# Graph network layers, one core: third tail column in a group of scatters, another place for the row table, weights split on ScalarE and GpSimd

## Chip, cores and metric

The kernel runs on one core of a Trainium2 chip. The metric is the device time of one launch in microseconds, the median of several runs. The engines are TensorE (PE), VectorE (DVE), ScalarE (ACT), GpSimd (POOL) and SyncE (SP), with 16 DMA engines that move data for all of them.

## What is computed

A graph has 3125 nodes with 64 features and 100000 weighted edges `src -> dst`, sorted by `dst`. Four graph layers follow each other, each on `h = relu(layernorm(x))`, and each adds its result to `x`:

```python
# layer 0: three propagations with deg^-1/2 on both sides, mean of four terms
msgs = x[row] * norm[:, None]
x = jax.ops.segment_sum(msgs, col, num_segments=num_nodes)
# layer 1: weighted mean over neighbours, two linear maps
msg = feat[src] * weight[:, None]
neigh_sum = jax.ops.segment_sum(msg, dst, num_segments=n)
rst = feat @ W_self.T + b_self + (h_neigh @ W_neigh.T + b_neigh)
# layer 2: Chebyshev filters of order 3 with symmetric normalisation, GRU gates
Z = sigmoid(_cheb_conv(X, src, dst, w, Wxz, bxz, n) + ...)
# layer 3: attention over the edges, 4 heads
att = exp(clip(einsum('ehd,ehd->eh', q, k), -10, 10))
out = segment_sum((att / attNorm)[:, :, None] * v, rows)
```

## The kernel before

**The idea.** The edges are turned into two dense matrices of 3200 x 3200 in device memory, one of edge counts and one of summed weights. After that every propagation is a product with one of them (`NPROP = 6` of these), and the attention layer uses the counts as well.

**First stage, tables.** `table` is an array of pairs (weight, count), one per cell, in tiles of 128 destination nodes (T = 25). The edges lie as columns of 128: edge `128 c + p` is in partition p of column c. A group is G = 10 columns; there are NG = 79 groups. Two edges of one cell may not be added by two lanes of the same scatter, so for each group DVE finds which edges are the last of their cell, and PE sums over the others:

- `make_row` (PE, L1136) spreads a group's keys over a row of 1280.
- `compare_own` (DVE, L772 to L784) compares each of the ten columns with the row and writes `equal`, then copies the weight parts (L780) and writes `is_row` (L782) and `is_tile` (L784).
- `compare_tail` (DVE, L764) compares the last TAIL = 2 columns of the group before with this group's row, all 1280 wide. What was still to be summed of these columns is carried on to this group.
- `add_up` (PE, L1119 to L1128) multiplies `equal` with the weight parts (three bf16 parts of an f32 weight, and a one for the count), and adds the carried amounts with `equal_tail` (L1128).
- `choose_cells` (DVE, L795 to L821) takes the sums and writes the cell numbers (L813) and amounts into one of SLOTS = 12 slots.
- `scatter` (POOL, L1350) issues one indirect DMA with addition per column.

DVE runs the loop one group behind itself: tail compare and own compare of group g, then the cells of group g-1. Over all groups but the first, `compare_tail` is called 78 times. After 14 and after 38 groups some other work of DVE stands between (first block L859 to L870, layer norm and weights).

**Order of the scatters.** Two scatters in flight may not touch the same cell. The first G - TAIL columns of a group are its body, the last TAIL its tail, each with its own semaphore:

```python
pool.wait_ge(body_landed, 16 * BODY * g)
scatter(slot, range(TAIL), body_landed)
previous_landed(g)          # waits for tail_landed, 16 * TAIL * g
scatter(slot, range(TAIL, BODY), body_landed)
scatter(slot, range(BODY, G), tail_landed)
```

So with TAIL = 2 a group begins when the body before it has landed, two scatters after the last of that body was issued, and its third column goes out when the tail before it has landed.

**Zeroing.** The table has to be zeroed tile by tile before it is added to. ACT issues four DMAs a tile (`zero_tile`, L504), the first ZEROED_AHEAD = 2 tiles at once one after the other, the rest as groups start.

**Splitting the table.** When enough groups have landed, ACT loads a tile (L526, 3.2 MB), splits it into weights and counts (L534, L537) and stores both (L546, 1.6 MB each). Tile 23 is copied by DVE into the ring (L946) and not only stored.

**Second stage, products.** SP streams pieces of the matrices (1.28 MB each) through a ring of five slots (`stream`, L452) and into places where they stay (`keep`, L458), PE multiplies (L1288, L1231, L1243), and DVE and ACT finish each block of columns. The ring lies where the first stage keeps keys, weights and parts, so SP waits with all of this for `scratch_read`, which DVE sets after its last group. The first two propagations go over blocks of four tiles each as far as tiles are stored.

**Third stage, attention.** Scores, exponentials, clip, product with the counts, sum over values: from about 1990 us on.

**The weights at the start.** The edge data come in rows and are transposed by PE (`turn_edges`, L1077): tiles, keys, rows, then weights. DVE copies each out of PSUM (`edges_of`, L713), and the copy is what frees the PSUM bank for PE (`edges_read`). The weights are copied to `w_e` and split into three bf16 parts in `parts` on DVE: cast, subtract, cast, subtract, cast (L735, L736, L742, L743, L756), with ones and a comparison for the count column (L757, L758).

Of the kernel before, what the change touches and what calls it, by code (L numbers as in the profile page):

```python
# [17 lines left out]
P = 128  # L18
# [6 lines left out]
NR = T * P  # L25
LAST = N - (T - 1) * P
G = 10
GE = G * P
NG = -(-E // GE)
ECP = NG * G  # L30
EDGE_TILES = -(-E // P)
WHOLE_TILES = E // P
REST = E - WHOLE_TILES * P
CHUNK_TILES = -(-ECP // P)
TAIL = 2
OWN_AT = [sum(G - i for i in range(j)) * P for j in range(G + 1)]
CELLS = NR * NR
TILE_CELLS = NR * P
ZEROED_AHEAD = 2
# [31 lines left out]
ALU = mybir.AluOpType  # L71
# [3 lines left out]
BF16 = mybir.dt.bfloat16  # L75
# [85 lines left out]
def carver(area):  # L161

    used = [0]

    def take(shape, dt):
        view, used[0] = carve(area, used[0], shape, dt)
        assert used[0] <= area.shape[1]
        return view

    return take  # L170


def tables_and_products(nc, c, k, sb, table, weights_dram, counts_dram, x_in, src, dst, edge_weight,
# [3 lines left out]
    def sem(name):  # L177
        return c.enter_context(nc.semaphore(name))
# [9 lines left out]
    ZEROS = 2 * NR // 4  # L188
# [9 lines left out]
    equal = [take([P, OWN_AT[G]], BF16) for b in range(2)]  # L198
    masks = take([P, P + GE], F32)
    take = carver(scaled_area)  # L200
    equal_tail, is_row = take([P, 2, TAIL, GE], BF16), take([P, 2, G, P], BF16)
    cells = k["held"][:, 0:2 * NR].rearrange("p (s c two) -> p s c two", c=P, two=2)
# [69 lines left out]
    needs_ready, group_started, group_taken = sem("needs_ready"), sem("group_started"), sem("group_taken")  # L272
    row_ready, first_keys = sem("row_ready"), sem("first_keys")
    masks_set, compared, tail_compared = sem("masks_set"), sem("compared"), sem("tail_compared")
    equal_ready, degrees_added = sem("equal_ready"), sem("degrees_added")
# [126 lines left out]
    with nc.Block() as block:  # L402
        @block.sync
        def _(sp):
# [5 lines left out]
            for tile, dram, landed in ((src_i, src, edges_landed), (dst_i, dst, edges_landed),  # L410
                                       (w_raw, edge_weight, weights_landed)):
                sp.dma_start(tile[0:LAST_ROWS, FILLED],
                             dram[FILLED * P * P:WHOLE_TILES * P].rearrange("(t e) -> t e", e=P)).then_inc(landed, 16)
                sp.dma_start(tile[LAST_ROWS:LAST_ROWS + 1, FILLED, 0:REST],
                             dram[WHOLE_TILES * P:E].rearrange("(a e) -> a e", a=1)).then_inc(landed, 16)
            sp.wait_ge(small_cleared, 3)
            small = [(k["x"][:, 0:T - 1, :], x_in[0:(T - 1) * P].rearrange("(t p) f -> p t f", p=P)),
# [12 lines left out]
            for to, frm in ((k["w_self"][row, :], b_self), (bias_in[row, 0:D], b_neigh),  # L430
                            (k["cheb0"][row, 0:D], bxz), (bias_in[row, D:2 * D], bhz),
                            (k["cheb0"][row, D:2 * D], bxh), (bias_in[row, 2 * D:3 * D], bhh)):
                sp.dma_start(to, frm.rearrange("(a f) -> a f", a=1)).then_inc(small_landed, 16)


            def tiles_stored(last_tile):
# [57 lines left out]
        def _(act):  # L494
# [5 lines left out]

            def zero_tile(t):
                for quarter in range(4):
                    cols = slice(quarter * ZEROS, (quarter + 1) * ZEROS)
                    act.dma_start(blocks[bass.ds(t, 1), :, cols].rearrange("a p c -> (a p) c"), zeros  # L504
                                  ).then_inc(quarter_zeroed, 16)
                act.wait_ge(quarter_zeroed, 64 * t + 64)
                act.sem_inc(tiles_zeroed, 1)

            for t in range(ZEROED_AHEAD):
                zero_tile(t)  # L510
            act.wait_ge(needs_ready, 4)
# [166 lines left out]
        def _(dve):  # L678
            steps = [0]

            def link(ins):

                steps[0] += 1
                ins.then_inc(dve_step, 1)
                dve.wait_ge(dve_step, steps[0])
# [10 lines left out]
            nc.vector.memset(masks[:, P:P + GE], 1.0).then_inc(masks_set, 1)  # L696
            link(nc.vector.memset(parts[:], 0.0))

# [12 lines left out]
            def edges_of(to, banks, n):  # L711
# [21 lines left out]
                                    ALU.is_ge, ALU.mult).then_inc(extremes_ready, 1)  # L733
            edges_of(w_e, totals, 4)
            link(nc.vector.tensor_copy(parts[:, :, 0], w_e[:]))  # L735
            link(nc.vector.tensor_tensor(w_e[:], w_e[:], parts[:, :, 0], ALU.subtract))  # L736
            dve.wait_ge(extremes_turned, 2)
# [3 lines left out]
                                    ).then_inc(extremes_ready, 1)  # L741
            link(nc.vector.tensor_copy(parts[:, :, 1], w_e[:]))  # L742
            link(nc.vector.tensor_tensor(w_e[:], w_e[:], parts[:, :, 1], ALU.subtract))  # L743
            nc.vector.tensor_scalar(schedule[:, 0], tiles_iota[0:1, :], float(LOAD_EVERY), float(LOADS_FROM),
# [10 lines left out]
            nc.vector.tensor_copy(tile_numbers, tiles_iota[:]).then_inc(masks_set, 1)  # L755
            nc.vector.tensor_copy(parts[:, :, 2], w_e[:])  # L756
            nc.vector.memset(parts[:, 0:WHOLE_TILES, 3:4], 1.0)  # L757
            link(nc.vector.tensor_scalar(parts[:, WHOLE_TILES, 3:4], partition[:], float(REST), None, ALU.is_lt))  # L758
            dve.wait_ge(masks_set, 4)
# [8 lines left out]

            def compare_own(g, b, more=True):

                for j in range(G):
                    ins = nc.vector.scalar_tensor_tensor(  # L772
                        equal[b][:, OWN_AT[j]:OWN_AT[j + 1]], key_row[b][:, j * P:GE], keys[:, bass.ds(g * G + j, 1)],
                        own_mask[:, 0:GE - j * P], ALU.is_equal, ALU.mult, accum_out=later[:, b, j:j + 1])
                if more:
                    ins = nc.vector.tensor_copy(keys_now[:, b], keys[:, bass.ds((g + 2) * G, G)])
                ins.then_inc(compared, 1)
                dve.wait_ge(row_ready, g + 2 if more else NG)
                edges = bass.ds(g * G, G)
                nc.vector.tensor_copy(parts_g[:, b], parts[:, edges, :])  # L780
                nc.vector.tensor_tensor(keys_rel[:, b], keys[:, edges], dummy[:], ALU.subtract)
                nc.vector.tensor_tensor(is_row[:, b], row_numbers.unsqueeze(1).to_broadcast([P, G, P]),  # L782
                                        dst_row[:, edges].unsqueeze(2).to_broadcast([P, G, P]), ALU.is_equal)
                nc.vector.tensor_tensor(is_tile[:, b], tile_numbers.unsqueeze(1).to_broadcast([P, G, T]),  # L784
                                        dst_tile[:, edges].unsqueeze(2).to_broadcast([P, G, T]), ALU.is_equal
                                        ).then_inc(equal_ready, 1)
# [40 lines left out]
            dve.wait_ge(row_ready, 1)  # L827
            compare_own(0, 0)
            dve.wait_ge(row_ready, 2)
# [497 lines left out]
        def _(pool):  # L1327
# [15 lines left out]
            nc.gpsimd.iota(partition[:], pattern=[[0, 1]], base=0, channel_multiplier=1,  # L1343
                           allow_small_or_imprecise_dtypes=True).then_inc(pool_step, 1)
            pool.wait_ge(needs_ready, 4)
            pool.wait_ge(dummies_zeroed, 16)
# [385 lines left out]
```

## Time and profile before

| | us |
|---|---|
| median of 3 runs | 2415.12 (2412.22 to 2417.41) |
| the profiled execution | 2415.37 |
| its span, first to last instruction | 2413.6 |
| DVE busy | 1786.2 (74%) |
| POOL busy | 1563.6 (65%) |
| PE busy | 1359.5 (56%) |
| ACT busy | 636.7 (26%) |

The span is what the trace shows of one execution; 1.8 us lie around it. Busy shares are means over three stages with different limits, so the text goes by stretches. DMA issues are not counted as busy for SP and ACT. In the rows, "ring", "resident", "scaled" and "held" are large areas of on-chip memory that hold different tables in different stages; `table` is the cell array.

### The profile page before, as it was taken

What the parts mean: (1) busy time and instruction counts of PE and PEld (TensorE: products, weight loads), DVE (VectorE), ACT (ScalarE), POOL (GpSimd) and SP (SyncE); (2) the same over time, 40 slices, a digit from 0 to 9 for tenths busy, and PEclk for the clock granted to TensorE, in tenths of its full rate; (3) what the DMA queues carried; (4) which work ended last, traced back from release to release, by engine and by line L of the source; (5) the groups of instructions that cost most, each with busy time, mean ns of one, the idle gap of its engine ahead of it and who ended that gap; (6) DMA issues with size and microseconds to landing.
All of it is one profiled execution on the core that took longest, in us unless ns stands there. A gap on an engine that the chain in (4) does not pass through costs nothing. (4 is left out here: it accounts for less than half of the span.)

```text
span 2413.6 us, 41312 instructions
## 1 busy us (share of the span) xinstructions
PE 1359.5 (56%) x13050; PEld 756.0 (31%) x13050; DVE 1786.2 (74%) x3954; ACT 636.7 (26%) x1822; POOL 1563.6 (65%) x1191
## 2 busy tenths in 40 slices
PE   2332223332332332333232577599999979999998
PEld 2222222222222222222222122143434443333334
DVE  8999999999999999999999000132321358999996
ACT  0000000012232331322111111010000237888884
POOL 1788888888888888888888777400000037888884
PEclk6555555555555555555555888799999988999997
DMA  5566666645666656664554999899998865333331
GB/s 202 164 163 192 183 170 164 164 109 164 181 167 198 164 164 204 175 167 116 142 124 80 339 372 346 300 375 360 395 397 298 323 179 160 106 104 104 106 107 50
DMA packets 253738, 481.44 MB, mean 199 GB/s; under 512 B 130710, under 2 KB 140093, under 8 KB 243933
## 3 DMA queue, kind: packets, MB, share of 16 engines
q1 hardware_dynamic: 113180, 229.09, 27.7%
q10 hardware_dynamic: 26000, 245.78, 25.5%
q0 software_dynamic: 114480, 5.67, 12.2%
q8 instruction: 33, 0.54, 0.1%
q14 instruction: 45, 0.36, 0.0%
HBM read 312.54 MB, written 167.91 MB: 199 GB/s over the span
## 5 line engine op out<-in xcount | busy, mean ns | idle before, releaser
L1350 POOL DMA_INDIRECT table<-held x782 | 1216.6, 1556 | 331.8 <-issue 305.9
L772 DVE SCALAR_TENSOR_TENSOR resident<-banks,ring,resident 128x1280 bf16<-128x1280 f32 (+9 forms) x790 | 694.3, 946 | 0.3 <-DVE ring L758 0.3
L1136 PE MATMUL banks<-ident,held 128*128 128x128 f32 x790 | 189.2, 426 | 866.0 <-DVE held L784 831.5
L1136 PEld LDWEIGHTS banks<-ident,held 128*128 128x128 f32 x790 | 157.6, 225 | 873.4 <-DVE held L784 838.1
L1545 DVE TENSOR_TENSOR att<-att,banks_d 128x1024 f32<-128x1024 f32 (+1 forms) x350 | 365.9, 1085 | 36.6 <-POOL att L1610 29.8
L1610 POOL TENSOR_SCALAR att<-att 128x1024 f32<-128x1024 f32 (+1 forms) x350 | 320.3, 934 | 85.8 <-ACT att L1513 85.8
L534 ACT ACTIVATE held<-held 128x128 f32<-128x128 f32 x575 | 172.0, 301 | 764.1 <-DMA weights_dram<-held 732.3
L1288 PE MATMUL banks<-ring,scaled 128*64 128x512 f32 x1120 | 297.4, 623 | 71.6 <-DMA ring<-counts_dram 50.0
L1513 ACT ACTIVATE att<-banks_d 128x1024 f32<-128x1024 f32 (+1 forms) x350 | 302.3, 915 | 79.8 <-PE banks_d L1633 79.8
L1398 POOL DMA_DIRECT2D parts_dram<-scaled x7 | 5.5, 779 | 380.1 <-DVE scaled L984 379.9
L764 DVE SCALAR_TENSOR_TENSOR scaled<-banks,ring,resident 128x1280 bf16<-128x1280 f32 x156 | 235.7, 1549 | 16.8 <-PE banks L1136 10.9
L1633 PE MATMUL banks_d<-held 96*128 (+2 forms) x700 | 170.2, 366 | 10.6 <-ACTq L1504 9.8
L1648 PE MATMUL banks_d<-att,v_tile 128*32 128x512 f32 (+1 forms) x1400 | 172.0, 567 | 0.5 <-DVE att L1545 0.5
L1288 PEld LDWEIGHTS banks<-ring,scaled 128*64 128x64 f32 x1120 | 91.3, 142 | 244.5 <-issue 186.8
L1119 PE MATMUL banks<-ring,resident 128*128 128x6 bf16 x4345 | 132.3, 167 | 24.5 <-DVE held L784 22.7
L1119 PEld LDWEIGHTS banks<-ring,resident 128*128 128x128 bf16 x4345 | 124.1, 104 | 33.9 <-DVE held L784 23.0
L517 ACT ACT_TABLE_LOAD x1 | 1.3, 1283 | 470.5 <-DMA table<-acc 470.5
L782 DVE TENSOR_TENSOR scaled<-banks,ring 128x1280 bf16<-128x1280 f32 x79 | 117.2, 1484 | 0.0
L1633 PEld LDWEIGHTS banks_d<-held 96*128 (+1 forms) x700 | 54.0, 99 | 182.0 <-issue 130.0
L534 ACT ACTIVATION_READ_ACCUMULATOR held<-held (+1 forms) x575 | 107.7, 187 | 0.0
L1640 PE MATMUL banks_d<-ident,count 128*128 128x128 f32 x625 | 102.6, 282 | 1.6 <-DVE att L1545 1.0
L1640 PEld LDWEIGHTS banks_d<-ident,count 128*128 128x128 f32 x625 | 79.2, 144 | 29.1 <-issue 8.9
(227 smaller groups left out, 1455.7 us busy)
## 6 DMA issues: line engine op xcount, KB each, us to landing
table<-acc ACTq DMA_DIRECT2D x100, 800.0 KB
held<-table ACTq DMA_DIRECT2D x24, 3200.0 KB
ring<-weights_dram SPq DMA_DIRECT2D x60, 1280.0 KB, 13.6
ring<-counts_dram SPq DMA_DIRECT2D x54, 1280.0 KB, 12.1
weights_dram<-held ACTq DMA_DIRECT2D x25, 1600.0 KB
counts_dram<-c_tile ACTq DMA_DIRECT2D x24, 1600.0 KB, 14.3
count<-counts_dram SPq DMA_DIRECT2D x150, 256.0 KB, 2.7
table<-held POOLq DMA_INDIRECT x782
```

Source lines behind the costliest of these rows:

```text
L534: ins = nc.scalar.activation(w_rows[:, s // PIECE, s % PIECE], cells[:, s, :, 0], ACT.Copy, accum_out=deg_parts[:, s, bass.ds(t, 1)])
L764: ins = nc.vector.scalar_tensor_tensor(equal_tail[:, b, i, :], key_row[b], keys[:, bass.ds(g * G - TAIL + i, 1)], all_mask, ALU.is_equal, ...
L772: ins = nc.vector.scalar_tensor_tensor(equal[b][:, OWN_AT[j]:OWN_AT[j + 1]], key_row[b][:, j * P:GE], keys[:, bass.ds(g * G + j, 1)], own_ ...
L1119: nc.tensor.matmul(sums, equal[b][:, at:at + P], parts_g[:, b, j, :], start=False, stop=True, skip_group_check=True)
L1136: ins = nc.tensor.transpose(key_row[b][:, j * P:(j + 1) * P], keys_now[:, b, j:j + 1].to_broadcast([P, P]), k["ident"][:])
L1288: ins = nc.tensor.matmul(sums, xs[:, prop % 2, s], rows_for(s), start=i < 2 and (prop != 1 or n == NC - 1), stop=True, skip_group_check=True)
L1350: nc.gpsimd.indirect_dma_start(out=table, out_offset=bass.IndirectOffsetOnAxis(ap=cell[:, slot, j:j + 1], axis=0), in_=amount[:, slot, j, ...
L1513: nc.scalar.activation(att[:, j, pairs[f], 0:W], scores[:, pairs[f], 0:W], ACT.Exp).then_inc(scores_read[f], 1)
L1545: ins = nc.vector.tensor_tensor(att[:, j, pairs[f], 0:W], att[:, j, pairs[f], 0:W], times, ALU.mult)
L1610: nc.gpsimd.tensor_scalar(att[:, j, pairs[f], 0:W], att[:, j, pairs[f], 0:W], HI, LO, ALU.min, ALU.max).then_inc(clipped[f], 1)
L1633: ins = nc.tensor.matmul(scores[:, hd, 0:W], k6[:, hd, bass.ds(t * P, P)], q6[:, hd, bass.ds(ci * BANK, W)], start=True, stop=True)
L1640: ins = nc.tensor.transpose(count_t[j % 3][:, s * P:(s + 1) * P], count[:, j, s, :], k["ident"][:])
```

## The change

TAIL goes from 2 to 3: `compare_tail` compares three columns per group, the body has seven scatters and the tail three, and the carried arrays have three columns. `is_row` moves from the area "scaled" to "resident", which makes room for the larger `equal_tail`. The copy of the weights and the casts into `parts` go to ACT, the subtracts, the ones and the comparison to POOL. PE's bank is freed by ACT after its second copy. The zeroing of tiles 0 and 1 goes to SP, ahead of its small loads.

```diff
-TAIL = 2
+TAIL = 3
...
+    is_row = take([P, 2, G, P], BF16)
     take = carver(scaled_area)
-    equal_tail, is_row = take([P, 2, TAIL, GE], BF16), take([P, 2, G, P], BF16)
+    equal_tail = take([P, 2, TAIL, GE], BF16)
...
+            sp.wait_ge(zeros_ready, 1)
+            for t in range(ZEROED_AHEAD):
+                for quarter in range(4):
+                    cols = slice(quarter * ZEROS, (quarter + 1) * ZEROS)
+                    sp.dma_start(table[0:CELLS].rearrange("(t p c) two -> t p (c two)", p=P, c=NR)[t, :, cols], zeros
+                                 ).then_inc(first_zeroed, 16)
             sp.wait_ge(small_cleared, 3)
...
+            sp.wait_ge(first_zeroed, 64 * ZEROED_AHEAD)
+            sp.sem_inc(tiles_zeroed, ZEROED_AHEAD)
...
-                act.wait_ge(quarter_zeroed, 64 * t + 64)
+                act.wait_ge(quarter_zeroed, 64 * t - 64 * (ZEROED_AHEAD - 1))
                 act.sem_inc(tiles_zeroed, 1)
 
-            for t in range(ZEROED_AHEAD):
-                zero_tile(t)
+            act.wait_ge(edges_turned, 4)
+            turned_weights = totals.rearrange("p a r -> p (a r)")[:, 0:ECP]
+            nc.scalar.copy(w_e[:], turned_weights).then_inc(weights_cast, 1)
+            act.wait_ge(parts_cleared, 1)
+            nc.scalar.copy(parts[:, :, 0], turned_weights).then_inc(weights_cast, 1)
+            act.wait_ge(weights_cast, 2)
+            act.sem_inc(edges_read, 1)
+            for n in range(1, 3):
+                act.wait_ge(weights_left, n)
+                nc.scalar.copy(parts[:, :, n], w_e[:]).then_inc(weights_cast, 1)
+            act.wait_ge(tiles_zeroed, ZEROED_AHEAD)
             act.wait_ge(needs_ready, 4)
...
-            edges_of(w_e, totals, 4)
-            link(nc.vector.tensor_copy(parts[:, :, 0], w_e[:]))
-            link(nc.vector.tensor_tensor(w_e[:], w_e[:], parts[:, :, 0], ALU.subtract))
...
-            link(nc.vector.tensor_copy(parts[:, :, 1], w_e[:]))
-            link(nc.vector.tensor_tensor(w_e[:], w_e[:], parts[:, :, 1], ALU.subtract))
...
-            nc.vector.tensor_copy(parts[:, :, 2], w_e[:])
-            nc.vector.memset(parts[:, 0:WHOLE_TILES, 3:4], 1.0)
-            link(nc.vector.tensor_scalar(parts[:, WHOLE_TILES, 3:4], partition[:], float(REST), None, ALU.is_lt))
...
+                if first:
+                    dve.wait_ge(ones_parted, 2)
+                    dve.wait_ge(weights_cast, 4)
                 nc.vector.tensor_copy(parts_g[:, b], parts[:, edges, :])
...
-            compare_own(0, 0)
+            compare_own(0, 0, first=True)
...
+            pool.wait_ge(parts_cleared, 1)
+            nc.gpsimd.memset(parts[:, 0:WHOLE_TILES, 3:4], 1.0).then_inc(ones_parted, 1)
+            pool.wait_ge(ones_parted, 1)
+            nc.gpsimd.tensor_scalar(parts[:, WHOLE_TILES, 3:4], partition[:], float(REST), None, ALU.is_lt
+                                    ).then_inc(ones_parted, 1)
+            for n in range(2):
+                pool.wait_ge(weights_cast, n + 2)
+                nc.gpsimd.tensor_tensor(w_e[:], w_e[:], parts[:, :, n], ALU.subtract).then_inc(weights_left, 1)
             pool.wait_ge(needs_ready, 4)
```

On DVE, ahead of the first compare, before (names: "held" has the schedule here, "ring" the parts of the weights):

```order
L753 SCALAR_TENSOR_TENSOR held<-banks,held 1x25
L755 COPY banks<-held 128x25
L756 CAST ring<-ring 128x790
L757 MEMSET ring 128x781
L758 TENSOR_SCALAR ring<-held 128x1
L772 SCALAR_TENSOR_TENSOR resident,held<-banks,ring,resident 128x1280
```

and now:

```order
L769 TENSOR_SCALAR held<-held 1x25
L771 SCALAR_TENSOR_TENSOR held<-banks,held 1x25
L773 COPY banks<-held 128x25
L787 SCALAR_TENSOR_TENSOR resident,held<-banks,ring,resident 128x1280
L787 SCALAR_TENSOR_TENSOR resident,held<-banks,ring,resident 128x1152
```

The cast and the two fills (like five more rows further up) are gone from DVE; the first compare follows the small schedule steps directly.

On DVE within a group, from `is_tile` to the cell numbers, before (`x2` is the tail compare):

```order
L784 TENSOR_TENSOR held<-banks,ring 128x250
L764 SCALAR_TENSOR_TENSOR scaled,held<-banks,ring,resident 128x1280 x2
L795 TENSOR_TENSOR deg_in<-deg_in,banks 128x25
L797 TENSOR_REDUCE held<-banks 128x20
L802 SCALAR_TENSOR_TENSOR held<-held 128x4
L807 TENSOR_TENSOR held<-held 128x2
```

and now:

```order
L802 TENSOR_TENSOR held<-banks,ring 128x250
L779 SCALAR_TENSOR_TENSOR scaled,held<-banks,ring,resident 128x1280 x3
L813 TENSOR_TENSOR deg_in<-deg_in,banks 128x25
L815 TENSOR_REDUCE held<-banks 128x20
L820 SCALAR_TENSOR_TENSOR held<-held 128x6
L825 TENSOR_TENSOR held<-held 128x3
```

One tail compare is added, and the carry steps have six and three elements in place of four and two.

## Rows read from the trace of the kernel before

**Rows 1.** The page's slices: busy tenths and GB/s in 40 equal slices.
```profile
DVE  8999999999999999999999000132321358999996
...
DMA  5566666645666656664554999899998865333331
GB/s 202 164 163 192 183 170 164 164 109 164 181 167 198 164 164 204 175 167 116 142 124 80 339 372 346 300 375 360 395 397 298 323 179 160 106 104 104 106 107 50
```

**Rows 2.** The page's costliest groups: busy us, mean ns of one, idle before.
```profile
L1350 POOL DMA_INDIRECT table<-held x782 | 1216.6, 1556 | 331.8 <-issue 305.9
L772 DVE SCALAR_TENSOR_TENSOR resident<-banks,ring,resident 128x1280 bf16<-128x1280 f32 (+9 forms) x790 | 694.3, 946 | 0.3 <-DVE ring L758 0.3
...
L764 DVE SCALAR_TENSOR_TENSOR scaled<-banks,ring,resident 128x1280 bf16<-128x1280 f32 x156 | 235.7, 1549 | 16.8 <-PE banks L1136 10.9
```

**Rows 3.** Timeline of POOL: start us, us, instruction, idle time before it.
```profile
51.92 1.85 POOL L1350 DMA_INDIRECT table<-held  x1 [47.42 <-issue]
...
96.19 1.55 POOL L1350 DMA_INDIRECT table<-held  x1 [2.97 <-issue]
...
1330.56 1.55 POOL L1350 DMA_INDIRECT table<-held  x1 [1.82 <-DMA table<-held]
...
1527.45 1.55 POOL L1350 DMA_INDIRECT table<-held  x1 [6.09 <-issue]
1529.30 1.55 POOL L1350 DMA_INDIRECT table<-held  x1 [0.30 <-issue]
...
1549.43 1.55 POOL L1350 DMA_INDIRECT table<-held  x1 [3.72 <-issue]
```

**Rows 4.** Timeline of DVE, the cell numbers of groups 2, 77 and 78.
```profile
94.39 0.17 DVE L813 TENSOR_TENSOR held<-held 128x10 f32 x1 [0.17 <-DVE held L810]
...
1303.23 0.17 DVE L813 TENSOR_TENSOR held<-held 128x10 uint32<-128x10 f32 x1
...
1321.83 0.17 DVE L813 TENSOR_TENSOR held<-held 128x10 uint32<-128x10 f32 x1
```

**Rows 5.** Timeline of DVE, first and last step of the block between groups.
```profile
273.18 1.82 DVE L859 TENSOR_REDUCE stat<-x_nodes 128x25 f32<-128x1600 f32 x1
...
282.13 0.23 DVE L870 TENSOR_TENSOR halves_sum<-ident 128x64 f32<-128x64 f32 x1
```

**Rows 6.** Timeline of SP: the first loads of the counts, merged.
```profile
1321.89 92.10 SPq L452 DMA_DIRECT2D ring<-counts_dram  x20
1414.10 23.18 SPq L458 DMA_DIRECT2D resident<-counts_dram  x4
1441.99 66.85 SPq L452 DMA_DIRECT2D ring<-counts_dram  x14
```

**Rows 7.** Windows: length, busy us of each engine, PE clock, DMA share, GB/s.
```profile
1300.00:1555.00 255.00, 149.37 (x689) 52.13 (x691) 39.92 (x96) 35.45 (x157) 182.44 (x118) 0.76 0.96 314
1555.00:1920.00 365.00, 348.72 (x1862) 153.43 (x1860) 96.21 (x253) 37.65 (x73) 0.00 (x0) 0.99 0.94 352
```

**Rows 8.** Timeline around PE's wait for tile 23.
```profile
1528.80 0.35 ACTq L526 DMA_DIRECT2D held<-table  x1
...
1545.49 1.98 PE L1288 MATMUL banks<-ring,scaled 128*64 128x512 f32 x4 [15.77 <-DVE ring L946]
```

**Rows 9.** Timeline of DVE: a wait for PE in group 1, and two tail compares.
```profile
66.89 0.18 DVE L795 TENSOR_TENSOR deg_in<-deg_in,banks 128x25 f32<-128x25 f32 x1 [2.46 <-PE banks L1128]
...
1304.63 1.54 DVE L764 SCALAR_TENSOR_TENSOR scaled<-banks,ring,resident 128x1280 bf16<-128x1280 f32 x1
...
1306.10 1.55 DVE L764 SCALAR_TENSOR_TENSOR scaled<-banks,ring,resident 128x1280 bf16<-128x1280 f32 x1
```

**Rows 10.** Timeline of DVE: the first cast of the weights, the first compare.
```profile
22.25 1.48 DVE L735 CAST ring<-ring 128x790 bf16<-128x790 f32 x1
...
33.37 1.55 DVE L772 SCALAR_TENSOR_TENSOR resident<-banks,ring,resident 128x1280 bf16<-128x1280 f32 x1 [0.29 <-DVE ring L758]
```

**Rows 11.** A copy on ACT (timeline) and the clip on POOL (the page's groups).
```profile
1504.33 3.08 ACT L537 COPY c_tile<-held 128x3200 f32<-128x3200 f32 x1
...
L1610 POOL TENSOR_SCALAR att<-att 128x1024 f32<-128x1024 f32 (+1 forms) x350 | 320.3, 934 | 85.8 <-ACT att L1513 85.8
```

More of the change, by code:

```diff
@@ L273, in tables_and_products @@
     row_ready, first_keys = sem("row_ready"), sem("first_keys")
+    parts_cleared, ones_parted = sem("parts_cleared"), sem("ones_parted")
+    weights_cast, weights_left = sem("weights_cast"), sem("weights_left")
+    first_zeroed = sem("first_zeroed")
     masks_set, compared, tail_compared = sem("masks_set"), sem("compared"), sem("tail_compared")
@@ L696, in _ @@
             nc.vector.memset(masks[:, P:P + GE], 1.0).then_inc(masks_set, 1)
-            link(nc.vector.memset(parts[:], 0.0))
+            nc.vector.memset(parts[:], 0.0).then_inc(parts_cleared, 1)
             dve.wait_ge(edges_landed, 16 * 6)
@@ L767, in compare_tail, with compare_own @@
                 ins.then_inc(tail_compared, 1)
-            def compare_own(g, b, more=True):
+            def compare_own(g, b, more=True, first=False):
                 for j in range(G):
```

## The prediction

> **What bounds the kernel now.** I read the page's slices first: VectorE (DVE) is busy at 9 tenths up to the 22nd of 40 slices, and the DMA share jumps to 9 where DVE falls to nothing [rows 1]. A slice is 60 us, so both happen near 1320 us. The costliest groups say what runs until then: 782 scatters on GpSimd (POOL), the compares on DVE [rows 2]. I then took three timelines.
>
> First, the scatters. One is 1.55 us and the next starts 0.30 after its end [rows 3], 1.856 us in all, so a group of ten takes 18.56 us. The first starts at 51.92, the last but one at 1549.43 [rows 3], so POOL is done near 1553. 782 x 1.856 is 1451 us, so of these 1501 only some 50 are waits beyond the 0.30. They lie in two places: four before 140 us (the second is the one at 96.19), and twelve from 1330.56 to 1549.43, in nearly every case one a group, up to 6.09 us [rows 3]. Between them POOL never waits.
>
> Second, DVE. The sum that writes a group's cell numbers (L813), on which its scatters wait, is at 94.39 for group 2 and 1303.23 for group 77 [rows 4]. Less a block of other work in between (273.18 to 282.36, 9.2 us [rows 5]) that is (1208.8 - 9.2) / 75 = 16.0 us a group. So DVE gains 2.56 us a group on POOL.
>
> Third, the handover. DVE's last such sum is at 1321.83 [rows 4], and SyncE issues the first load of the count matrix at 1321.89 [rows 6]: the ring that these loads fill holds the keys that DVE compares, so **the stream begins when DVE has finished**, while POOL still scatters. From there DMA is the limit: its share is 0.96 in 1300:1555 at 314 GB/s [rows 7], by slice 339, 372, 346 and 300 GB/s, against 395 and 397 in later slices without scatters [rows 1]. After 1555 DMA (share 0.94, 352 GB/s) and TensorE (PE, 348.72 of 365 us busy) are both nearly full [rows 7]. Only once do they stand still for another reason: PE waits 15.77 us, until 1545.49, for DVE's copy (L946) of tile 23, which waits for that tile's load, issued at 1528.80 [rows 8]. That load waits for scatters. These 15.8 us are all the slack between the two paths: POOL's path ends last there, DVE's and the stream's come 16 us before it.
>
> **The change, part by part.**
>
> *Third tail column on DVE.* compare_tail runs 78 times (156 compares, two each [rows 2]) and gets one more compare of 128x1280. Their starts lie 1.47 us apart (1304.63, 1306.10) although each is shown as 1.55 [rows 9], so it costs 78 x 1.47 = 114.7 us of DVE. For group 1 DVE waits 2.46 us for PE at 66.89 [rows 9], which hides 1.1 of the 1.47 (PE's ten more matmuls a group take some of it back; they are small and overlap: I take 0.4). The carry steps have 6 elements in place of 4, nothing. Sum +113.6 us; with 1.55 for each it would be +120. The group takes 16.0 + 1.47 = 17.47 us, still under POOL's 18.56, by 1.09. DVE's lead at its end shrinks to some five groups, so the twelve slots never hold it up.
>
> *The weights.* Off DVE go a copy, three casts and two subtracts of 790 columns and two short fills, eight steps before the first compare at 33.37; the first cast takes 1.48 us from 22.25 on [rows 10]. Some 9 us of DVE go, and the small steps left between them (1.5 us) need PE's answers and PE's row of keys (ten transposes) as before. PE also waits until ScalarE (ACT) has copied the weights twice. No copy of 790 columns is there on ACT; 3200 take 3.08 us [rows 11], so 0.8 us each, or double if half of it is a fixed part. The first of them can start where DVE's copy did, a microsecond before 22.25. 21.2 + 2 x 0.8 (to 1.6) + 2.4 for the row gives a first compare at 25.2 to 26.8: I take **-7 us** (between -6 and -8.5). Two subtracts on POOL and two casts on ACT must then be done when DVE copies the parts, after its ten compares of the group, which by the mean of 0.946 us [rows 2] come to 9 us. POOL clips 1024 columns in 0.93 us [rows 11]; two inputs may cost it twice as much, so 2 x 1.6 + 2 x 0.8 and some handovers are near 6 us: hidden. If a POOL step took 4 us, some 2 us would come back.
>
> *Zeroing of tiles 0 and 1 by SyncE*: the same 8 DMAs go out on another queue, behind the edges, and no longer one tile after the other. Both tiles are 6.4 MB, 21 us even at the 300 GB/s of the slowest of the four slices named above, and the first scatter starts at 51.92 [rows 3]: nothing. The small loads queued behind them are not used until 273 us [rows 5]. *is_row moves* inside on-chip memory, same shape: nothing, as all work there stays on DVE and PE.
>
> *Scatters.* The first comes 7 - 1.5 = 5.5 us earlier. Group 2 was already waited for on DVE's side (L813 at 94.39, scatter at 96.19 [rows 3, 4]); it moves to about 94.39 - 7 + 1.47 + 0.4 + 1.47 = 90.7, so 3.7 earlier only. In each group the waits for the body and for the tail now come three scatters after the last of these, not two: 1.86 us more cover. That takes up to 3.7 from the third and fourth wait. Of the twelve late waits the six before 1428 (the first is that at 1330.56, together 14.8 us beyond the 0.30 [rows 3]) stand beside the stream, which isn't there yet, and should go; the six after can lose 11 at most, and I take half. POOL ends near 1553 - 3.7 - 3.7 - 14.8 - 5 = 1526, within 1520 to 1545.
>
> Here a rule speaks against the third column. The body's last scatter is the eighth of ten, so the group that starts at 1527.45 sends it at 1527.45 + 7 x 1.856 = 1540.44, and the next group may go on at 1549.43 [rows 3]: from its end a landing took 7.4 us there, and no more than the 4.0 of two scatters and a gap where POOL never waits. The Trainium skill (DMA: Bandwidth & Descriptors, Anatomy of one DMA) puts a DMA started by GpSimd at a fixed 2.0 us or so. By that rule two scatters of distance would always do, and the scatter term would be 0; the trace agrees with it from 140 to 1330 us and contradicts it at both ends.
>
> *The stream.* It now starts at 1321.9 - 7 + 113.6 = **1428**. From 1321.9 up to PE's restart at 1545.5 it must bring 20 + 4 + 11 full pieces of 1.28 MB (the 14 issued from 1441.99 hold 3 short ones), 1.5 MB of short ones, one for c_tile and the first 0.96 of tile row 5: 48.6 MB [rows 6]. Besides, each tile costs a load and a store of 3.2 MB. From 1428 to 1525 at 360 GB/s, amid the four slices, DMA moves 35 MB; two loads and two stores take 12.8, so 22 MB of stream. Left are 26.4, with a load and a store 33 MB, at the 395 GB/s of a slice without scatters [rows 1] 83 us: PE restarts at 1608 in place of 1545.5, **+62 us**. Since tile 24 is then long there, PE's small waits behind it and the last loads beside it should fall away, -5. All later work shifts with it: PE has 16 us of idle in the next 365 [rows 7].
>
> **Sum:** -7 + 113.6 on DVE is 106.6; 15.8 of it is the old slack; some 29 come from less traffic beside the stream (12.8 MB of tile traffic done before 1428) and the higher rate once the scatters end; 5 behind it: +57. The profiled execution took 2415.4 (span 2413.6 and 1.8 around it), 0.3 over the median of 2415.1. Forecast 2415.1 + 57 = **2472 us**.
>
> **Rivals.**
> - *Full delay.* The stream keeps its old pace, 314 to 350 GB/s with the same gaps: +106.6 - 15.8 = +91, 2506. For: DMA's share is full already at the low rates. Against: a quarter of the old traffic in that stretch is gone. 0.13.
> - *More is caught up.* PE uses the 16 us of idle after 1555 and DMA runs at 395 all along: 67.8 MB in 172 us is a restart at 1600, +54, less 16 and 5: +33, 2448. Against: both engines would have to be full at once. 0.13.
> - *DVE becomes the bound of the scatters too.* The margin is 1.09 us a group. If the new group took 19.5 us (PE's answers later, POOL and DVE in each other's way), the stream would start at 1428 + 78 x 2.0 = 1584, with hardly any scatter or tile traffic beside it: 48.6 MB at 395 in 123 us put PE's restart at 1707 and the end at 2415 + 162 - 5 = 2572. Against: one compare more needs nothing new of PE. 0.03.
> - *Faster:* POOL's end alone sets the end, and the stream catches up in full. Then the 28 us that the scatters end earlier are the gain, less the part that falls behind: 2390 to 2413. Decides if 48.6 + 12.8 MB move between 1428 and 1517, 690 GB/s; the highest slice shows 397 [rows 1]. 0.03.
> - *No change* (within 0.2%, about what runs of this kernel can tell): the stream's slack is far larger than the 16 us seen, because DMA moves the same bytes at a higher rate when they are asked for later. PE's 149.37 busy us in 1300:1555 [rows 7] would nearly fit into what is left, the bytes don't. 0.02.
>
> **How the numbers follow.** Forecast 0.66. The range takes in both neighbours: low 2440 (a bit under 2448, for a start 2 us better and POOL's end at 1520), high 2508 (full delay). Outside are 0.03 above, 0.05 below, and some of the neighbours' spread. Slower 0.95, same 0.02, faster 0.03.
>
> **What would show it.** 234 tail compares; SyncE's first count load near 1428; the last scatter near 1525; no wait over 3 us of POOL from 140 to 1428; PE's restart with tile row 5 near 1608, waiting for the ring and not for DVE's copy of tile 23; everything from there 365 us long as before. If PE still waits there for DVE's copy, the stream had slack that I don't see, and the time is near or under the old one. If DVE's group is over 18.6 us, the third rival holds.

## The result, and the profile after

The changed kernel takes **2507.6 us** (median of 4, 2506.53 to 2509.18) against 2413.7 (2408.99 to 2417.41) for the kernel before: ratio 1.0387, 95% interval 1.0375 to 1.0399. Slower, as forecast, but by 94 us where 57 were forecast. That is the value of the rival "full delay" (2506), and it lies 0.4 us inside the upper end of the range (2508), which was set by that rival. The profiled execution's span is 2505.2 (before 2413.6).

The page's slices of the changed kernel (a slice is 62.6 us), as in [rows 1]:

```profile
DVE  8999999999999999999999800032221157999996
...
DMA  6566576546656657554442399998999785333332
GB/s 194 158 198 169 158 210 158 158 105 187 181 158 194 174 158 210 158 158 105 105 105 1 77 360 381 342 372 331 395 397 346 291 261 150 106 105 105 107 107 52
```

VectorE is busy up to the 23rd slice now. New is the hole ahead of the stream: 1 GB/s in the 22nd slice and 77 in the 23rd, which ends with the stream's first pieces. No tile is loaded, split or stored there.

The costliest groups of the changed kernel, as in [rows 2]:

```profile
L1376 POOL DMA_INDIRECT table<-held x782 | 1212.7, 1551 | 311.2 <-issue 286.2
...
L787 DVE SCALAR_TENSOR_TENSOR resident<-banks,ring,resident 128x1280 bf16<-128x1280 f32 (+9 forms) x790 | 694.1, 945 | 3.7 <-PE banks L1154 3.7
L779 DVE SCALAR_TENSOR_TENSOR scaled<-banks,ring,resident 128x1280 bf16<-128x1280 f32 x234 | 350.4, 1547 | 14.9 <-PE banks L1154 10.9
```

234 tail compares cost 350.4 us in place of 235.7 for 156: 114.7 more, the very sum forecast.

The timeline of VectorE, cell numbers of groups 2, 76, 77 and 78, as in [rows 4] (groups are numbered from 0, so 78 is the last):

```profile
92.42 0.17 DVE L831 TENSOR_TENSOR held<-held 128x10 f32 x1 [0.17 <-DVE held L828]
...
1407.76 0.17 DVE L831 TENSOR_TENSOR held<-held 128x10 uint32<-128x10 f32 x1
1424.77 0.17 DVE L831 TENSOR_TENSOR held<-held 128x10 uint32<-128x10 f32 x1
1427.76 0.17 DVE L831 TENSOR_TENSOR held<-held 128x10 uint32<-128x10 f32 x1
```

The last is 105.9 us later than before. A group takes (1407.76 - 92.42 - 9.2) / 74 = 17.65 us. Counted back from the last one, the 1303.23 of [rows 4] was group 76's and not 77's, so the group before took 1208.8 - 9.2 over 74, 16.2 us, and the margin to POOL is now 0.9 us.

The timeline of SyncE, the stream, as in [rows 6]:

```profile
1427.82 128.43 SPq L465 DMA_DIRECT2D ring<-counts_dram  x20
1556.36 14.97 SPq L471 DMA_DIRECT2D resident<-counts_dram  x4
1575.17 51.47 SPq L465 DMA_DIRECT2D ring<-counts_dram  x14
```

It begins where forecast (1428), but the first 20 pieces take 128.4 us in place of 92.1. Beside them four tiles are now loaded and four stored; before, it was two loads and one store.

The timeline of ScalarE's queue, tile loads (the last ahead of the hole, then tiles 20 to 23) and the step between them:

```profile
1251.93 0.35 ACTq L549 DMA_DIRECT2D held<-table  x1
...
1427.67 0.21 ACT L592 COPY w_neigh<-banks 128x64 f32<-128x64 f32 x1 [137.05 <-PE banks L1180]
1428.72 0.41 ACTq L549 DMA_DIRECT2D held<-table  x1
1464.13 0.35 ACTq L549 DMA_DIRECT2D held<-table  x1
1499.30 0.35 ACTq L549 DMA_DIRECT2D held<-table  x1
...
1533.31 0.35 ACTq L549 DMA_DIRECT2D held<-table  x1
```

This is what the forecast missed. Between tile 19's split and tile 20's load, ScalarE's program has a block of other work: two copies of layer weights that PE turns when VectorE's groups are over, then the square root of the degrees. ScalarE waited 137 us for it. In the kernel before, the same wait was 27.2 us, and tile 20's load came out 12 us behind it, when enough scatters had landed; the block didn't hold it, since run 10, without the block ahead of it, has the load at 1333.82. The timeline of ScalarE before:

```profile
1321.74 0.21 ACT L569 COPY w_neigh<-banks 128x64 f32<-128x64 f32 x1 [27.23 <-PE banks L1162]
...
1333.69 0.35 ACTq L526 DMA_DIRECT2D held<-table  x1
```

The timeline of GpSimd, the starts of groups from 1428 on, as in [rows 3]:

```profile
1444.03 1.54 POOL L1376 DMA_INDIRECT table<-held  x1 [8.46 <-issue]
...
1454.80 1.54 POOL L1376 DMA_INDIRECT table<-held  x1 [5.53 <-DMA table<-held]
...
1485.80 1.54 POOL L1376 DMA_INDIRECT table<-held  x1 [12.80 <-DMA table<-held]
...
1526.11 1.54 POOL L1376 DMA_INDIRECT table<-held  x1 [9.16 <-issue]
...
1554.94 1.54 POOL L1376 DMA_INDIRECT table<-held  x1 [10.63 <-issue]
1556.79 1.55 POOL L1376 DMA_INDIRECT table<-held  x1 [0.30 <-issue]
```

There are five waits of 5.5 to 12.8 us where there were six of 2.1 to 6.1, although each has a scatter more of cover. The four waits at the start did not shrink either: 15.4 us in sum, before 12.8. POOL ends at 1558, not at 1526.

PE's restart with tile row 5, the copy of tile 23 that it waits for (the timeline, as in [rows 8]) and the windows, as in [rows 7] (length, busy us of PE, PE's weight loads, DVE, ACT and POOL, PE clock, DMA share, GB/s):

```profile
1632.16 4.46 PE L1261 MATMUL banks<-ring,scaled 128*64 128x512 f32 x10 [2.91 <-DMA ring<-counts_dram]
...
1636.72 3.49 DVE L964 COPY ring<-held 128x3200 f32<-128x3200 f32 x1 [38.25 <-PE banks L1261]
...
1640.31 11.52 PE L1306 MATMUL banks<-ring,scaled 128*64 128x512 f32 x40 [3.68 <-DVE ring L964]
```

```profile
1427.00:1640.00 213.00, 128.51 (x493) 42.81 (x490) 16.25 (x37) 35.43 (x157) 72.27 (x47) 0.80 1.01 363
...
1640.00:2010.00 370.00, 354.35 (x1882) 155.25 (x1884) 97.64 (x252) 37.65 (x73) 0.00 (x0) 0.99 0.94 354
```

PE still waits for DVE's copy, but only for its 3.7 us; the copy itself waited 38 us for PE's earlier products (L1261), and the last of these waited for a piece of the stream. The forecast's sign for slack in the stream, PE waiting for the copy, was badly chosen: the copy waits in its turn. It is the stream that sets the restart, 94.8 us later than before. From there to the end it is 864.9 us (before 868.1).

The same stretch of the kernel before, from the start of its stream to its restart, as windows:

```profile
1321.00:1545.00 224.00, 134.61 (x496) 44.02 (x493) 16.27 (x37) 35.45 (x157) 160.99 (x105) 0.78 1.05 353
```

224 us at 353 GB/s are 79.1 MB; 213 at 363 are 77.3. **The stretch carries nearly the same bytes as before**, with four tile loads and four stores in each; some 2 MB are fewer.

### The profile page after: what moved, and what is told of

Read it like the earlier page. It is cut to its first block and busy times, and to the rows that moved or that the text cites. A ratio compares the mean times of both kernels' runs of the same rounds, so it can differ in the third digit from the quotient of the medians.

```text
span 2505.2 us, 43099 instructions
## 1 busy us (share of the span) xinstructions
PE 1364.8 (54%) x13830; PEld 771.5 (31%) x13830; DVE 1893.7 (76%) x4102; ACT 647.0 (26%) x1827; POOL 1567.9 (63%) x1195
## 5 line engine op out<-in xcount | busy, mean ns | idle before, releaser
L779 DVE SCALAR_TENSOR_TENSOR scaled<-banks,ring,resident 128x1280 bf16<-128x1280 f32 x234 | 350.4, 1547 | 14.9 <-PE banks L1154 10.9
L1137 PE MATMUL banks<-ring,resident 128*128 128x6 bf16 x4345 | 128.9, 167 | 25.2 <-DVE held L802 25.2
L800 DVE TENSOR_TENSOR resident<-banks,ring 128x1280 bf16<-128x1280 f32 x79 | 117.0, 1481 | 0.0
L625 ACT COPY scaled<-banks 128x512 f32<-128x512 f32 (+1 forms) x35 | 18.9, 539 | 312.0 <-PE banks L1306 312.0
```

The source lines that it names most:

```text
L779: ins = nc.vector.scalar_tensor_tensor(equal_tail[:, b, i, :], key_row[b], keys[:, bass.ds(g * G - TAIL + i, 1)], all_mask, ALU.is_equal, ...
L1137: nc.tensor.matmul(sums, equal[b][:, at:at + P], parts_g[:, b, j, :], start=False, stop=True, skip_group_check=True)
```

## The experiments

The common idea behind them is that VectorE's end starts the stream, and that what lies beside the stream sets how fast it catches up.

**1. ScalarE's block later** (the changed kernel, one edit):

```diff
+            pass_on(T // 4 - 2, 3)
+            pass_on(T // 4 - 1, 0)
             act.wait_ge(turned_ready, 1)
...
-            pass_on(T // 4 - 2, 3)
-            for j in range(2):
-                pass_on(T // 4 - 1, j)
+            pass_on(T // 4 - 1, 1)
```

> The changed kernel, but ScalarE's wait for VectorE's last group (turned_ready, deg_ready, three small steps) stands after two more tiles are passed on, so that loads and stores of tiles 20 and 21 are not queued behind it. Theory A: in the changed kernel these loads (first one issued at 1428.7, when VectorE ended) fell into the stream and slowed it; here the load of tile 20 is issued near 1325, SyncE's first 20 pieces take 100 us in place of 128, PE's restart after its early pieces moves from 1640 to about 1612, and the time is 2480 us (2470 to 2490). Rival B: the stream beside scatters is slow whatever ScalarE does, and the loads only change places: 2503 to 2510.

Measured: 2484.3 us (2483.85 to 2486.64), ratio 1.0289 (1.0272 to 1.0306). Its timeline of ScalarE, then its windows and PE's restart:

```profile
1324.08 0.35 ACTq L549 DMA_DIRECT2D held<-table  x1
...
1379.66 0.35 ACTq L549 DMA_DIRECT2D held<-table  x1
...
1427.60 0.21 ACT L594 COPY w_neigh<-banks 128x64 f32<-128x64 f32 x1 [9.30 <-PE banks L1180]
1438.95 0.39 ACTq L549 DMA_DIRECT2D held<-table  x1
...
1502.97 0.35 ACTq L549 DMA_DIRECT2D held<-table  x1
```

```profile
1427.00:1617.00 190.00, 127.35 (x492) 44.37 (x490) 16.65 (x38) 14.27 (x55) 70.63 (x46) 0.82 0.96 335
```

```profile
1616.96 10.03 PE L1306 MATMUL banks<-ring,scaled 128*64 128x512 f32 x30 [3.68 <-DVE ring L964]
```

Two tiles are loaded and two stored in what was the hole: 190 us at 335 GB/s are 63.7 MB, 13.6 fewer than in the changed kernel. PE restarts at 1617, POOL's late waits are 4.6 us at most and its last scatter ends at 1525, the value forecast. The first 20 pieces take 106.5 us (100 were expected). The hold of ScalarE's queue cost 23.3 us of the 94. The rate fell with the bytes: 13.6 MB at 363 GB/s would be 37 us, and only 23 came back.

**2. Only tile 20's load ahead of the block** (the changed kernel; `pass_on` of tile 19 is taken apart):

```diff
+            split_done(KEPT_OUT - 4)
+            load(KEPT_OUT - 3)
             act.wait_ge(turned_ready, 1)
...
-            pass_on(T // 4 - 2, 3)
+            store(KEPT_OUT - 4, 1)
+            split(KEPT_OUT - 3, 0, 2 * (T // 4 - 2) + 2)
```

> The changed kernel with that same edit: tile 20's load near 1324 in place of 1428.7, but tile 19's store, tile 21's load and tile 20's store still behind the block, as in the changed kernel. 3.2 of the 12.8 MB that the earlier move took out of the stream's stretch. If the loss is a matter of bytes moved into that stretch, a quarter to a third of the 23.3 us comes back: 2499 to 2503. Rival: the chain of load, split and store per tile sets the pace of tile 23 and so counts by tiles, one of two is half of it: 2494 to 2498.

Measured: 2498.97 us (2498.12 to 2501.47), ratio 1.0348 (1.0334 to 1.0362). By its windows:

```profile
1427.00:1633.00 206.00, 125.16 (x486) 41.79 (x488) 16.81 (x38) 35.45 (x157) 69.56 (x46) 0.81 1.01 360
```

74.2 MB, 3.1 fewer than in the changed kernel, and 8.6 us less time, for one of the four transfers (3.2 MB each) that run 1 moved. That is 37% of run 1's gain, between the two expectations (2499 to 2503 by bytes, 2494 to 2498 by tiles), just below the first. The restart, at 1632.90, is 7.4 us earlier, a third of run 1's 23.3. So the bytes explain it better than the count of tiles, but the two are not told apart cleanly.

**3. Two columns again, all else as changed** (`TAIL = 2` in the changed kernel).

> The changed kernel with TAIL back at 2: the parts of the change on the weights, the row table and the zeroing alone. Theory: first compare 3.5 us earlier as in the changed kernel (29.9 against 33.4), first scatter near 47, and as the path over the scatters sets PE's restart here, the gain comes through: 2409 to 2412 us. Rival: the gain is lost in the wait of group 2 or later: 2413 to 2415.

Measured: 2405.8 us (2404.72 to 2406.93), ratio 0.9959 (0.9945 to 0.9973): 3 us better than the best expected. The third column is the whole loss, 101.8 us against this run; what else was changed leaves 10 us of gain. Its stream starts only 1 us earlier than in the kernel before (1320.95), 106.9 us ahead of the changed kernel's, but tile 23 is loaded at 1520.32 in place of 1528.80, and PE's 15.8 us of waiting for its copy [rows 8] are 3.7 (more of PE's waiting now lies ahead of it, for pieces of the ring):

```profile
1543.17 13.81 PE L1306 MATMUL banks<-ring,scaled 128*64 128x512 f32 x49 [3.68 <-DVE ring L964]
```

The restart is only 2.3 us earlier; most of the gain falls behind it (861.7 us to the end, before 868.1). Which of the parts gives that, no run separates.

**4. Three columns alone** (the kernel before with `TAIL = 3` and `is_row` moved).

> The kernel before with TAIL = 3 and the row table moved to make room, nothing else. Theory: all of the loss is here: VectorE ends 3.5 us later than in the changed kernel (1431), time 2509 to 2513 us. Rival: the weights' new places cost something later on, then this is under 2505.

Measured: 2521.2 us (2518.39 to 2523.66), ratio 1.0442 (1.0424 to 1.0459). Outside what was expected: VectorE's end is at 1439.3, 11.5 us later than in the changed kernel. 3.65 of it are the first compare (33.52 for 29.87). Two waits with no releaser stand in its timeline of VectorE, at the first instruction of a round of twelve groups, and not in the changed kernel's:

```profile
939.11 1.55 DVE L765 SCALAR_TENSOR_TENSOR scaled<-banks,ring,resident 128x1280 bf16<-128x1280 f32 x1 [3.70 <-issue]
...
1157.45 1.55 DVE L765 SCALAR_TENSOR_TENSOR scaled<-banks,ring,resident 128x1280 bf16<-128x1280 f32 x1 [7.42 <-issue]
```

These 11.1 us and the 3.65 are 3.3 more than the 11.5; what gives the 3.3 back is open, and so is what the two waits are. From PE's restart (1651.45) to the end it is 865.0 us, as in the changed kernel.

**5. Three columns compared, scatters split 8 + 2** (`BODY = G - 2` in the changed kernel): the cover that the third column buys is given back.

> The changed kernel (three columns compared), but the scatters' own split is two columns again: body of eight, tail of two. Theory: the scatters are not what the end waits for in the changed kernel, so the time stays at 2505 to 2510 us; the waits before group starts grow by up to 1.86 us each, four early ones and five late ones, and the last scatter ends 5 to 17 us later than 1558. Rival: the waits are set by how fast DMA works off the scatters, not by the distance: same waits in sum, same end of the scatters within 3 us.

Measured: 2506.3 us (2504.27 to 2507.39), ratio 1.0378 (1.0361 to 1.0396): the same. POOL's waits beyond 0.30, without the first, add up to 71.6 us against 59.4, and its last scatter starts at 1566.28, 9.5 us later; the restart is at 1637.66, no later at all (1640.31 in the changed kernel). Of the 12.2 us of longer waits 2.3 lie before 180 us, the rest beside the stream. So the cover works on POOL, and POOL is off the path.

**6. The reverse: two compared, split 7 + 3** (`BODY = G - 3` in the kernel before).

> The kernel before (two columns compared), but the scatters are split as in the changed one, body of seven and tail of three, so the waits come three scatters after the last of their kind. Left out: what protects the third last column of a group against the same cell in the next group, so some sums may be lost; the number and size of the scatters is the same. Theory (a wait is a landing time less the distance): each of the waits, four early and about ten late, shrinks by up to 1.86 us; the last scatter ends 10 to 20 us before 1553, tile 23 is loaded earlier, and as PE's restart was set by that: 2402 to 2410 us. Rival (DMA works the scatters off at its own pace beside the stream): end of the scatters within 4 us, 2413 to 2416 us.

Measured: 2409.8 us (2407.61 to 2413.58), ratio 0.9982 (0.9973 to 0.9992). The last scatter starts 15 us earlier (1536.03) and tile 23's load 11 us earlier:

```profile
1517.74 0.35 ACTq L526 DMA_DIRECT2D held<-table  x1
```

PE's wait for the copy is gone from its timeline; now it waits for the ring:

```profile
1542.44 8.45 PE L1288 MATMUL banks<-ring,scaled 128*64 128x512 f32 x30 [4.75 <-DMA ring<-counts_dram]
```

That is what the longer distance alone gains in this kernel: about 5 us, with no third compare to pay for.

**7. One column compared** (the kernel before; `for i in range(TAIL - 1, TAIL)`, the left-out row zeroed once).

> The kernel before with one tail compare per group in place of two. Left out: the carry from the second last column (its equal_tail is zero throughout). Theory: VectorE ends 113 us earlier, near 1209, and the stream starts there, but PE's restart still waits for tile 23, which the scatters set (1545); the time moves by under 15 us: 2402 to 2416. Rival: VectorE's end sets the time as it stands, in this direction too: 2320 to 2380.

Measured: 2408.2 us (2403.86 to 2409.64), ratio 0.9969 (0.9958 to 0.998). The time is as expected, VectorE's end is not: 1308, not 1209. From group 57 on it waits for the slots:

```profile
917.78 0.18 DVE L795 TENSOR_TENSOR deg_in<-deg_in,banks 128x25 f32<-128x25 f32 x1 [1.96 <-POOLq L1367]
...
936.42 0.18 DVE L795 TENSOR_TENSOR deg_in<-deg_in,banks 128x25 f32<-128x25 f32 x1 [3.42 <-POOLq L1367]
```

These two are 18.6 us apart, POOL's pace. With twelve slots VectorE can't be further ahead. The stream starts 13.7 us earlier, and PE then waits 37.84 us for tile 23.

**8. GpSimd's ones later** (run 3, with a wait for the turned edges ahead of the fill): `pool.wait_ge(edges_turned, 4)`.

> The changed kernel with TAIL = 2 and GpSimd's fill of the ones (2.69 us at 7.5 in the changed kernel, beside a VectorE step of 2.96 us that took 0.63 before) put behind the transposes of the edges. Theory: GpSimd's fill holds VectorE up; the step is 0.63 again, the first compare comes 2.0 to 2.3 us earlier (27 in place of 29.1), and of it 1 to 2.3 us arrive at the end: 2403 to 2405 us against 2405.8. Rival: the step is slow for another reason (DMA writing the edges), no change. Either way GpSimd's fill then lies beside other VectorE steps and may stretch one of these.

Measured: 2405.1 us (2403.8 to 2405.86), ratio 0.9961 (0.9947 to 0.9974). The first compare is at 26.89 in place of 29.11 (25.2 to 26.8 were forecast); the total is not told apart from run 3.

**9 and 10. The block later with two columns**: run 1's edit on run 8 and on the kernel before.

> The version with two tail columns and the late fill of ones, with the move of ScalarE's block that gave 23 us with three. With two columns ScalarE waited 36.3 us for the block's product, until 1320.73, and issued tile 20's load at once behind it, at 1322.03. Theory (the load is held by the block): it is issued some 10 us sooner, near 1310, before the stream begins at 1318.7; a part of its 3.2 MB leaves the stretch of the stream, up to 8 us, of which the waits of PE for the ring can take back most: 2397 to 2404. Rival (nothing of it is on the path, since PE's restart hangs on later tiles): 2404 to 2406.

> The kernel before with the same move of ScalarE's block alone. There ScalarE waited 27.2 us, until 1321.74, but tile 20's load went out only at 1333.69, 11 us behind the block: it waited for scatters, so the block held nothing up. Theory: the time is the same, 2412 to 2417, and the 23 us of the same edit in the changed kernel are a cost that only the third compare brings. Rival (the hold was part of the old time too): 2400 to 2410.

Both expectations were wrong. Measured: 2460.0 us (2456.2 to 2461.84), ratio 1.0184 (1.0171 to 1.0198), for run 9, and 2471.3 us (2470.9 to 2472.27), ratio 1.0232 (1.0218 to 1.0246), for run 10. The timelines of ScalarE, of SyncE and of PE in run 10:

```profile
1428.13 0.20 ACT L571 COPY w_neigh<-banks 128x64 f32<-128x64 f32 x1
```

```profile
1322.14 197.88 SPq L452 DMA_DIRECT2D ring<-counts_dram  x20
```

```profile
1429.81 14.62 PE L1288 MATMUL banks<-ring,scaled 128*64 128x512 f32 x60 [107.86 <-DVE scaled L902]
```

The block's square root scales the operand of PE's first large product (L902). Moved behind tile 21's load, which waits for scatters, it came 106 us late; the ring filled and stood. The same edit gains 23 us with three columns and costs 55 (run 9) and 56 us (run 10) with two: with three, VectorE's end (1427.8) comes after tile 20's store anyhow, with two it comes at 1322.

**11. Only tile 20's load ahead of the block, two columns** (run 2's edit on run 8).

> The version with two tail columns and the late fill of ones; on ScalarE only tile 20's load goes ahead of the block, the block stays ahead of tile 19's store. The product of the propagation needs the block's square root, so it must not wait for tile 21 (that cost 108 us of TensorE in the run with the whole block moved). Tile 20's load goes out near 1317.7, the block's product is there at 1318.5 and nothing else is held up. Theory: PE's first large product starts within 1 us of where it did, and the time is 2402 to 2406, 0 to 4 less than without the edit. Rival (the load beside the first pieces of the stream hurts): 2406 to 2410.

Measured: **2403.1 us** (2400.75 to 2406.87), ratio 0.9947 (0.9934 to 0.9961), as expected. It is faster than the kernel before by 0.5% and than the changed one by 4%; the step from run 8 (2405.1) is within what the runs scatter.

## Why the forecast was right in sign and short in size

- *The step that failed: the stream, +62 at the restart.* It measured +94.8. The forecast moved 48.6 MB of stream and three tile loads and stores, 67.8 MB, in 180 us, at 377 GB/s, and put 12.8 MB of tile traffic down as "done before 1428". Measured are 77.3 MB in 213 us: nothing was done ahead, since four loads and four stores came after 1428. The 9.5 MB too few are 26 us at the measured 363 GB/s, and 67.8 MB at 363 and not 377 are 7 more; that makes the 33 us by which the restart came late. Of the 9.5 MB 6.4 are the fourth load and store; for the other 3.1 the sum has no term (SyncE had issued five more pieces by 1637.6, where it counts the first 0.96 MB). The loads were misplaced because I took them to follow the scatters and did not ask what else ScalarE's queue waits for; the wait of 27 us in the trace of before was the sign.
- *What runs show of this step.* The hold of the queue is worth 23.3 us (run 1) of the 35.6 by which the forecast fell short. The rest is mainly the rate: run 1 moved 63.7 MB, less than the forecast's 67.8, and still needed 190 us, at 335 GB/s. Why the rate falls when there is less beside the stream, no run separates; the DMA share was 0.96 there, and 1.01 in the changed kernel.
- *VectorE's end, +106.6.* It measured 105.9, but by luck: two terms were too large and cancel. The third column was put at +113.6; the compares take 114.7 more, but the changed kernel's stream starts only 106.9 us behind run 3's. Three kinds of small steps (L835, L791, L798) take 83.6 us with three columns and 93.5 with two; why is not shown. The start was put at -7. The first compare came 3.5 us earlier, and in run 3 only 0.9 of it is left where the stream starts.
- *Why -3.5 and not -7 at the first compare.* The casts were priced at 0.8 us from a plain copy [rows 11], and the first took 2.8; the fill on GpSimd held a step of VectorE (below). In run 8 it was -6.5. The steps that follow were hidden, as said.
- *Group time.* A group was 16.2 us and not 16.0, from a miscount of the group in [rows 4]. The margin over POOL still held (17.65 against 18.56), so the rival in which VectorE bounds the scatters did not come.
- *Scatters.* "The six before 1428 should go": they did, and from 140 us up to there no wait is over 3.00. "The six after can lose 11" was wrong: there are five, and they grew to 5.5 to 12.8 us each, since four tile loads and four stores were packed beside them. Run 1, with two of each gone, ends at the forecast 1525.
- *The Trainium skill's fixed 2.0 us* (DMA: Bandwidth & Descriptors, Anatomy of one DMA) would make the distance between scatters worth nothing. In runs 5 and 6 one scatter of distance is worth 9.5 and 15 us of POOL's time, most of it beside the stream, so the rule does not hold there.
- *-5 behind the restart*: 3.2.
- *The rivals.* "Full delay" gave the right time, by its own sum (+106.6 - 15.8), and for a reason close to its own: the stretch repeats the old one with nearly all its bytes. Its "against", that a quarter of the old traffic is gone, was the error. The range held only because it reached up to this rival; the forecast's own working did not lead there. "More is caught up" needed 395 GB/s all along; not even 377 came. The "faster" rival falls with runs 5 and 6: POOL's end is worth some 5 us.

## What to carry to other kernels

When an engine's end is moved, list every queue that waits for it, not only the one on the path: in-order queues of other engines may hold a small late block ahead of large transfers, and a wait that cost nothing before grows by the whole shift. Where such a block belongs depends on which of its two neighbours comes first: the same move was worth -23 us in one version and +56 us in another, so follow both what it holds up and who needs it. Forecast a bandwidth-bound stretch by its bytes from the trace, load by load, and at the rate of a stretch with the same mix.

## What the runs showed of the hardware

**Some of VectorE's steps stand while GpSimd fills.** The timelines of GpSimd and of VectorE in the changed kernel:

```profile
7.53 2.69 POOL L1364 MEMSET ring<- 128x781 bf16 x1 [3.02 <-DVE ring L720]
```

```profile
7.75 2.96 DVE L723 TENSOR_SCALAR ring<-ring 128x896 int32<-128x896 int32 x1 [0.27 <-DMA ring<-in_dst_dram]
```

The step takes 0.63 us before and in run 8. In run 8 the fill is elsewhere and stretches two steps of 25 elements, 0.16 us each in the changed kernel, which end with it (20.87 + 2.70 = 23.57). The steps L758 to L760, which read from PSUM ("banks"), run beside the same fill in 0.22 to 0.23 us, as in the changed kernel:

```profile
20.87 2.70 POOL L1365 MEMSET ring<- 128x781 bf16 x1 [16.36 <-PE banks L1095]
```

```profile
22.16 0.22 DVE L760 TENSOR_REDUCE held<-banks 25x1 f32<-25x79 f32 x1
22.30 1.30 DVE L762 TENSOR_SCALAR held<-held 1x25 f32<-1x25 f32 x1
22.38 1.24 DVE L764 TENSOR_SCALAR held<-held 1x25 f32<-1x25 f32 x1
```

The Trainium skill (SBUF — State Buffer, SBUF: two separate sides) has the port pair that the two share as an exclusive lock, held for a whole instruction by whichever starts first, and on VectorE's side it names only operations of certain kinds. The trace agrees: each of the three stretched steps ends 0.03 to 0.5 us after the fill whatever its size, and others are not touched. Which kind each step is, the trace does not say. So work given to GpSimd to relieve VectorE is not free where the two overlap.

**A cast with a strided target on ScalarE** costs in this kernel 3.4 times a plain copy of as many columns (each sixth bf16 element is written):

```profile
23.83 0.82 ACT L525 COPY ring<-banks 128x790 f32<-128x790 f32 x1 [14.32 <-PE banks L1095]
24.54 2.78 ACT L527 CAST ring<-banks 128x790 bf16<-128x790 f32 x1
```

Whether it is the stride or the type, no run here separates.
